# The lower form of the inverse's first level: by a mask and the preceding token's beta in place of sixteen products with the unit matrix

## The chip, the cores and the metric

The kernel runs on one core of one Trainium2 chip. The metric is the device time of one execution in microseconds. Three executions of the kernel before took 4968.78, 4977.33 and 4977.47 us; their median, 4977.33 us, is the time before.

## What is computed

Two transformer layers over 4096 tokens of width 256. Layer 0 adds a gated delta rule attention (16 heads of 64) and a mixture of 16 experts to its input; layer 1 adds a linear attention and a nested attention. Only the delta rule is touched by the change. For each head, with state `S` (64x64) and, per token, key `k`, query `q`, value `v`, log decay `g` and step size `beta = sigmoid(x @ Wb.T)`:

```
Sk    = einsum('bhkv,bhk->bhv', S, k_t)
delta = v_t (x) k_t - Sk (x) k_t
S     = exp(g_t) * S + b_t * delta
o_t   = einsum('bhkv,bhk->bhv', S, q_t)
```

The tokens of a head depend on each other in turn. The kernel takes them in chunks of 64: within a chunk the updates solve a triangular system, so a 64x64 triangular matrix (unit diagonal, off it the products of keys, the decays between two tokens and a beta) has to be inverted for each head and each chunk, and then the state goes from chunk to chunk.

## The kernel before, in words

The program runs in six phases, one after the other: norm and router, projections, delta rule (`phase_delta`), experts, second norm, attention. Each phase gives every engine a list of its own; engines meet only at semaphores, and each works its list strictly in order.

`phase_delta` has 64 chunks of 64 tokens. Two chunks make a couple, `x` = 0 and 1, and there are 32 couples. A tile is 128 partitions by 8 pairs of heads by 64 columns (128x512 f32): a head is a 64x64 square in the upper or the lower half of the partitions, so a product over all heads of a chunk is a block of sixteen matmuls (`heads()`, `each()`); a profile shows such a block as 32 weight loads and 32 matmuls of 64x64.

A round of the loop, `one(post, pre, ahead)` of each engine, works on three couples at once. For `ahead`, SP loads keys, queries, values and running sums of the decays (`load`, L758), and the decays are exponentiated. For `pre` the inverse is built (which needs no state). For `post` the state goes through its two chunks: `residual`, `updates`, `outputs`, `new_state`, then `project`. The loop's body holds two rounds. In all 32 rounds have a `pre`, 31 of them a `post` as well.

The inverse is built by doubling. `inv[x]` holds the inverse in its upper form, the transpose of it is the lower form, and both are needed since a matmul takes its left operand transposed. Level one (within pairs of neighbouring tokens) is made from `upper` by GpSimd: `first_inverse` (L1103) multiplies with the mask `couples` and subtracts from the unit matrix, two operations a chunk. Its lower form was made by TensorE: `first_low` (L819) multiplies `inv[x]` with the unit matrix into `p_low`, one block a chunk, and ScalarE's `keep_low` (L960) copies `p_low` to `inv_low[x]`. Each further level k = 1 to 4 is then, for each chunk: `half` (L825: `upper` by `inv_low` into `p_pre`), `mask_step` (L1038, VectorE, into `step`), `low` (L830: adds to what stands in `p_low`), `up` (L836: into `p_pre`), and then `keep_low` (ScalarE) and `add_up` (L1042, VectorE: `inv` plus `p_pre`). Level five has no lower form. `half(x, k + 1)` waits for the lower form of level k and for `add_up(x, k)`, which frees `p_pre`.

TensorE's order in a round is written out by hand (L875 to L918): keys by keys, residual 0, keys by keys, keys by queries, key rows 0, updates 0, keys by queries, key rows 1, outputs 0, `first_low(0)`, new_state 0, `first_low(1)`, `half(0, 1)`, `half(1, 1)`, residual 1, and then the levels, each `low 0, up 0, low 1, up 1, half 0`, one of updates 1, outputs 1, new_state 1 (levels 1 to 3), `half 1`. The last `up`s stand among two halves of `project`. VectorE's order is at L1052, ScalarE's at L964, GpSimd's at L1130, SP's at L776. `residual(post, 1)` waits for the state that VectorE's `take_state(post, 0)` (L1033) makes from new_state 0.

Of the kernel before, what the change touches and what calls it, by code (L numbers as in the profile page):

```python
# [24 lines left out]
C = 64  # L25
# [24 lines left out]
def shape_constants():  # L50

    p = np.arange(P)
    half, s = p // C, p % C
    t = np.arange(C)
    eye = np.eye(P)

    same_head = (half[:, None] == half[None, :]).astype(float)

    running = same_head * (s[:, None] <= s[None, :])
    tri = (s[:, None] <= t[None, :]).astype(float)  # L60
    future = np.where(tri > 0, 0.0, -1e30)


    doublings = []
    for n in range(LEVELS):
        w = 1 << n
        doublings.append((s[:, None] // (2 * w) == t[None, :] // (2 * w)) * (s[:, None] % (2 * w) >= w) * (t[None, :] % (2 * w) < w) * -1.0)
    couples = (s[:, None] // 2 == t[None, :] // 2) * (s[:, None] % 2 < 1) * (t[None, :] % 2 >= 1) * 1.0
    eye_c = (s[:, None] == t[None, :]).astype(float)
    parts = {  # L70
        "eye": eye, "same_head": same_head, "running": running, "future": future,
        "couples": couples, "doublings": np.concatenate(doublings[1:], 1), "eye_c": eye_c,
        "iota": np.tile(np.arange(NE), (P, 1)).astype(float),
        "head_block": (p[:, None] // DL == p[None, :] // DL).astype(float),
    }
# [567 lines left out]
def phase_delta(nc, g, ctx):  # L643
# [23 lines left out]
    k_t, q_t, v_t, sums = (sb(n, [P, 4, NPAIR, C]) for n in ("k_t", "q_t", "v_t", "sums"))  # L667
# [8 lines left out]
    inv_low = [sb(f"inv_low{x}", W) for x in range(2)]  # L676
    step = [sb(f"step{x}", W) for x in range(2)]
# [19 lines left out]
    wo_in, cleared = sem("wo_in"), sem("cleared")  # L697
    res_d, ress_d, w_d, u_d, udec_d, o_d, ocp_d = (sem(s) for s in ("res", "ress", "w", "u", "udec", "o", "ocp"))
# [56 lines left out]
    def _(sp):  # L755
        sp.dma_start(wo[:], g.given["wo_t"].rearrange("(n p) d -> p n d", p=P)).then_inc(wo_in, 16)

        def load(n, x):  # L758
            r, m = n.ring[x], n.chunk[x]
            for h in range(2):  # L760
                sp.dma_start(sums[h * C:(h + 1) * C, r].rearrange("p n t -> p (n t)"),
                             spread(g.sums_d[bass.ds(m, 1), h, :], [C, NPAIR * C])).then_inc(loaded[r], 16)
            for name, dst in (("k", k_t), ("q", q_t), ("v", v_t)):
                src = g.chunks_d[name][bass.ds(m, 1)].rearrange("a p n -> p (a n)")
                sp.dma_start(dst[:, r].rearrange("p n t -> p (n t)"), src).then_inc(loaded[r], 16)
# [10 lines left out]
        def one(post, pre, ahead):  # L776
            if ahead is None:
                return
            for x in range(2):
                if post is not None:  # L780
                    sp.wait_ge(o_d, post.ended[x])
                load(ahead, x)
            load_rows(ahead)
# [6 lines left out]
    def _(pe):  # L790
# [28 lines left out]
        def first_low(n, x):  # L819
            wait_apart(pe, g, (att_d[x], n.now), (inv1_d[x], n.now))  # L820
            for p, hs in heads():
                last = te.matmul(p_low[x][hs, p, :], inv[x][hs, p, :], g.c("eye_c")[hs, :], start=p == 0, stop=False, skip_group_check=True)
            last.then_inc(lowmm_d[x], 1)

        def half(n, x, k):  # L825
            freed = (rows_d[x], n.now) if k == 1 else (up_d[x], n.level[k - 1])
            wait_apart(pe, g, freed, (lowc_d[x], n.level[k]))
            each(p_pre[x], of(upper[x]), of(inv_low[x])).then_inc(half_d[x], 1)

        def low(n, x, k):  # L830
            wait_apart(pe, g, (step_d[x], n.level[k]))
            for p, hs in heads():
                last = te.matmul(p_low[x][hs, p, :], inv[x][hs, p, :], step[x][hs, p, :], start=False, stop=k == NL - 1, skip_group_check=True)  # L833
            last.then_inc(lowmm_d[x], 1)
# [40 lines left out]
        def one(post, pre, ahead):  # L875
# [15 lines left out]
            if pre is not None:  # L891
                first_low(pre, 0)
            if post is not None:
                new_state(post, 0)
            if pre is not None:
                first_low(pre, 1)
                half(pre, 0, 1)
                half(pre, 1, 1)
# [20 lines left out]

        couples(pe, one)  # L920

    @block.scalar
    def _(act):
# [3 lines left out]
        def grown(n, x):  # L927
# [6 lines left out]
            a.activation(grow[:, r, :, 1:], sums[:, r], ACT.Exp).then_inc(grow_d[x], 1)  # L934
# [25 lines left out]
        def keep_low(n, x, k):  # L960
            act.wait_ge(lowmm_d[x], n.level[k + 1])
            a.activation(inv_low[x][:], p_low[x][:], ACT.Copy).then_inc(lowc_d[x], 1)  # L962

        def one(post, pre, ahead):  # L964
# [7 lines left out]
            if pre is not None:  # L972
                keep_low(pre, 0, 0)
                keep_low(pre, 1, 0)
            if post is not None:
                keep_residual(post, 1)
            for k in range(1, NL):
                if pre is not None:
                    for x in range(2):
                        keep_low(pre, x, k)  # L980
                if post is not None and k == 2:
                    keep_outputs(post, 1)
# [15 lines left out]
    def _(dve):  # L998
        v = nc.vector
        v.memset(state[:], 0.0).then_inc(state_d, 1)  # L1000
        masks = g.c("doublings").rearrange("p (n t) -> p n t", n=NL)

        def decays(n, x):
# [3 lines left out]
            v.tensor_tensor(diff[x][:], sums[:, r], per_pair(g.cum, n.chunk[x]), ALU.subtract).then_inc(diff_d[x], 1)  # L1007
# [7 lines left out]
        def take_upper(n, x):  # L1015
            dve.wait_ge(kk_d[x], n.now)
            dve.wait_ge(relb_d[x], n.now)
# [20 lines left out]
        def mask_step(n, x, k):  # L1038
            dve.wait_ge(half_d[x], n.level[k])
            v.tensor_tensor(step[x][:], p_pre[x][:], over_pairs(masks[:, k - 1, :]), ALU.mult).then_inc(step_d[x], 1)  # L1040

# [10 lines left out]
        def one(post, pre, ahead):  # L1052
# [13 lines left out]
            for k in range(1, NL):  # L1066
                if pre is not None:
                    for x in range(2):
                        add_up(pre, x, k)
# [18 lines left out]
    def _(pool):  # L1088
# [3 lines left out]
        pool.wait_ge(cleared, 2)  # L1092

# [9 lines left out]
        def first_inverse(n, x):  # L1103
# [4 lines left out]
            po.tensor_tensor(inv[x][:], over_pairs(g.c("eye_c")), inv[x][:], ALU.subtract).then_inc(inv1_d[x], 1)  # L1108

# [20 lines left out]
        def one(post, pre, ahead):  # L1130
            if post is not None:
                decay_state(post, 0)
            if pre is not None:
                first_inverse(pre, 0)
                first_inverse(pre, 1)
            if post is not None:
                decay_updates(post, 0)
# [1230 lines left out]
```

## Time and profile before

| what | value |
|---|---|
| median of three executions | 4977.33 us |
| the profiled execution's own time | 4995.25 us |
| its span, first to last instruction | 4993.5 us |
| TensorE busy over the span | 4571.5 us (92%) |
| VectorE, ScalarE, GpSimd busy | 3236.5 (65%), 2104.2 (42%), 1165.6 us (23%) |
| delta rule phase, first to last matmul | about 731.9 to 2435 us |

Busy time of TensorE comes from matmuls whose ends are modelled, so a gap in it is a lower bound of a stall; the starts of weight loads (PEld) are the better clock of where TensorE stands. Behind a row in brackets stands how long the engine was idle before it and what released it.

### The profile page before, as it was taken

How to read it: one execution, taken by the hardware profiler on the slowest of the kernel's cores; microseconds unless marked ns; L12 is line 12 of the kernel's file. 1: busy time of each engine (PE TensorE's matmuls, PEld its weight loads, DVE VectorE, ACT ScalarE, POOL GpSimd, SP SyncE). 2: the span in 40 equal slices, each digit the busy share in tenths (PEclk: the TensorE clock that was granted, in tenths of full speed). 3: DMA queues.
4: the chain of work that ended last, by engine and by line, in shares of the span. 5: the costliest groups of instructions: out<-in, count | busy, mean ns of one | idle time of the engine just before them, and what ended most of it. 6: DMA issues, size and time to landing. Idle time of an engine off the chain costs nothing. (4 is left out here: it accounts for less than half of the span.)

```text
span 4993.5 us, 162520 instructions
## 1 busy us (share of the span) xinstructions
PE 4571.5 (92%) x67085; PEld 2950.8 (59%) x67085; DVE 3236.5 (65%) x5639; ACT 2104.2 (42%) x2965; POOL 1165.6 (23%) x1361
## 2 busy tenths in 40 slices
PE   6777759999999999999997777999999999999998
PEld 6333338999999998998764662444444444444443
DVE  4788874444444444444333896878787878787877
ACT  1566642222222222222133442656565656565654
POOL 1354442322322323223102774000000000000000
PEclk9998979999999999999998997999999999999999
DMA  3421241111111111111223333000000000000000
GB/s 106 137 101 71 80 145 44 44 54 53 47 52 52 52 55 44 52 55 44 64 85 113 106 104 76 8 9 14 17 4 17 4 17 4 17 5 18 9 13 8
DMA packets 201350, 250.07 MB, mean 50 GB/s; under 512 B 52864, under 2 KB 132864, under 8 KB 199968
## 3 DMA queue, kind: packets, MB, share of 16 engines
q1 hardware_dynamic: 180240, 209.29, 13.3%
q0 software_dynamic: 6144, 16.79, 1.1%
q10 hardware_dynamic: 14352, 14.55, 0.9%
q8 instruction: 538, 8.81, 0.7%
q14 instruction: 76, 0.62, 0.0%
HBM read 135.18 MB, written 105.38 MB: 48 GB/s over the span
## 5 line engine op out<-in xcount | busy, mean ns | idle before, releaser
L2154 DVE TENSOR_REDUCE part_max<-p_m 128x1 f32<-128x512 f32 x2118 | 1363.9, 686 | 378.8 <-PE p_m L1996 371.3
L2136 ACT ACTIVATE prob<-p_s 128x1024 f32<-128x1024 f32 x1024 | 1048.6, 1024 | 748.4 <-PE p_s L2060 746.5
L2015 PE MATMUL p_o<-prob,v_one 128*64 128x512 f32 x4096 | 1055.0, 593 | 3.9 <-ACT prob L2136 0.5
L1996 PE MATMUL p_m<-keys,queries 96*64 96x512 f16 x4236 | 661.3, 387 | 28.0 <-DMA keys<-parts_d 20.4
L2060 PE MATMUL p_s<-queries,keys 97*64 97x512 f16 x4096 | 618.9, 380 | 0.0
L2060 PEld LDWEIGHTS p_s<-queries,keys 97*64 97x64 f16 x4096 | 227.9, 109 | 599.4 <-issue 593.9
L1050 DVE TENSOR_TENSOR inv<-inv,pd_pre 128x512 f32<-128x512 f32 x256 | 176.2, 688 | 446.2 <-PE pd_pre L795 446.2
L544 PE MATMUL p_proj<-xn_t_all,proj_w_sb 128*128 (+1 forms) x768 | 390.2, 651 | 78.3 <-ACT raw L570 70.3
L962 ACT ACTIVATE inv_low<-pd_low 128x512 f32<-128x512 f32 x320 | 191.1, 597 | 621.1 <-PE pd_low L833 471.3
L795 PE MATMUL pd_pre<-inv,step 64*64 64x64 f32 x10240 | 395.3, 219 | 30.4 <-issue 27.5
L1996 PEld LDWEIGHTS p_m<-keys,queries 96*64 96x64 f16 x4236 | 238.5, 108 | 311.3 <-DVE part_max L2154 56.5
L1964 POOL TENSOR_TENSOR attn<-o_num,o_inv 32x512 f32<-32x512 f32 x64 | 81.2, 1269 | 1453.6 <-DVE o_inv L2173 1447.1
L795 PEld LDWEIGHTS pd_pre<-inv,step 64*64 64x64 f32 x10240 | 351.0, 135 | 68.8 <-issue 66.9
L2015 PEld LDWEIGHTS p_o<-prob,v_one 128*64 128x64 f32 x4096 | 287.5, 136 | 162.9 <-issue 15.9
L795 PE MATMUL pd_pre<-inv_low,upper 64*64 64x64 f32 x10240 | 367.6, 219 | 11.8 <-issue 11.5
L795 PEld LDWEIGHTS pd_pre<-inv_low,upper 64*64 64x64 f32 x10240 | 340.3, 135 | 18.1 <-issue 15.3
L607 DVE SCALAR_TENSOR_TENSOR conv<-raw,conv_w_sb,conv 128x512 f32<-128x512 f32 x384 | 312.4, 813 | 57.0 <-POOL raw L631 45.3
L544 PEld LDWEIGHTS p_proj<-xn_t_all,proj_w_sb 128*128 128x128 f32 x768 | 155.5, 208 | 304.1 <-issue 178.3
L1040 DVE TENSOR_TENSOR step<-pd_pre,const 128x512 f32<-128x512 f32 x320 | 218.2, 690 | 159.7 <-PE pd_pre L795 157.9
L833 PE MATMUL pd_low<-step,inv 64*64 64x64 f32 x8192 | 298.8, 218 | 2.6 <-issue 2.4
L833 PEld LDWEIGHTS pd_low<-step,inv 64*64 64x64 f32 x8192 | 275.4, 135 | 4.6 <-issue 3.7
L1101 POOL TENSOR_TENSOR upper<-rel,beta 128x512 f32<-128x512 f32 x64 | 66.7, 1042 | 669.2 <-ACT rel L943 669.2
(240 smaller groups left out, 6624.5 us busy)
## 6 DMA issues: line engine op xcount, KB each, us to landing
k_d<-qkv SPq DMA_DIRECT2D x8, 2048.0 KB, 7.5
q_d<-qkv SPq DMA_DIRECT2D x8, 2048.0 KB, 12.3
v_d<-qkv SPq DMA_DIRECT2D x8, 2048.0 KB, 7.3
sums<-sums_d SPq DMA_DIRECT2D x128, 128.0 KB, 2.9
k_t<-k_d SPq DMA_DIRECT2D x64, 256.0 KB, 3.2
q_t<-q_d SPq DMA_DIRECT2D x64, 256.0 KB, 3.4
v_t<-v_d SPq DMA_DIRECT2D x64, 256.0 KB, 4.7
slots_d<-zero ACTq DMA_DIRECT2D x1, 10112.0 KB, 31.9
```

Of the source, the lines that this page charges most:

```text
L544: last = te.matmul(p_proj[j % RING][:], g.proj_w_sb[:, n, c, p * P:(p + 1) * P], g.xn_t[:, c, bass.ds(b * BLK, BLK)], start=c == 0, stop=c ...
L607: v.scalar_tensor_tensor(rows, cols, w, rows, ALU.mult, ALU.add).then_inc(conv_d, 1)
L795: last = te.matmul(out[hs, p, :], lhs(p, hs), rhs(p, hs), start=True, stop=True)
L833: last = te.matmul(p_low[x][hs, p, :], inv[x][hs, p, :], step[x][hs, p, :], start=False, stop=k == NL - 1, skip_group_check=True)
L962: a.activation(inv_low[x][:], p_low[x][:], ACT.Copy).then_inc(lowc_d[x], 1)
L1040: v.tensor_tensor(step[x][:], p_pre[x][:], over_pairs(masks[:, k - 1, :]), ALU.mult).then_inc(step_d[x], 1)
L1050: v.tensor_tensor(inv[x][:] if k < NL else inv_fin[:, n.ring[x]], inv[x][:], p_pre[x][:], ALU.add).then_inc(up_d[x], 1)
L1996: last = te.matmul(p_m[k % 2][x * HALF:(x + 1) * HALF, :], queries[0:ROW, p, hh, at:at + HALF], keys[0:ROW, 2 * p + hh, kb * BLK:(kb + 1) ...
L2015: product = te.matmul(p_o[64 * hh:64 * hh + VW, :], g.v_one[:, j, p, hh:hh + 2, :].rearrange("p a d -> p (a d)"), prob[:, j % 2, hh, :], s ...
L2060: last = te.matmul(p_s[j % 2][x * HALF:(x + 1) * HALF, hh, :], keys[0:KR, 2 * p + hh, at:at + HALF], queries[0:KR, p, hh, :], start=True, ...
L2136: a.activation(prob[:, j % 2], p_s[j % 2][:], ACT.Exp, scale=SCORE_SCALE).then_inc(exp_d, 1)
L2154: v.tensor_reduce(part_max[:, hh * SUB + sub, kb:kb + 1], p_m[k % 2][:], AX.X, ALU.max).then_inc(red_d, 1)
```

## The change

The lower form of level one is no longer taken from the upper form. Its only entries off the diagonal are those of a token and the one before it, in which the decay is the factor of the upper form's own and only the beta is of another place. So VectorE masks the product of keys with itself (`couples_low`, -1 at the places) from `p_pre` into a new tile `low_1[x]`; GpSimd multiplies it by `beta_before`, the beta of the token preceding, and adds the unit matrix.

- TensorE: `first_low` is gone (two blocks a round); `half(0, 1)` stands in its first place, and `half(1, 1)` alone stands between new_state 0 and residual 1. `low(x, 1)` now begins the accumulation in `p_low`.
- VectorE: `take_upper` has the masking ahead of its own operation; `add_low` (levels 1 to 4, ahead of each `add_up`) adds `low_1` and `p_low` into `inv_low`.
- ScalarE: all of `keep_low` is gone (five a chunk); `keep_outputs(1)` follows `keep_residual(1)`.
- GpSimd: `first_low` (two operations a chunk) stands where `first_inverse` was, and `first_inverse` comes after `decay_updates(post, 0)`.
- Once, ahead of the loop: one matmul shifts beta by a token, VectorE copies it, and TensorE and GpSimd wait for that.
- `sums` has two places in place of four, so SP's loads wait for the decays and growths of the couple before.
- The constants have 192 more columns (64 for `couples_low`, 128 for `previous`).

```diff
@@ shape_constants
+    couples_low = (s[:, None] // 2 == t[None, :] // 2) * (s[:, None] % 2 >= 1) * (t[None, :] % 2 < 1) * -1.0
+        "couples_low": couples_low, "previous": (p[:, None] == p[None, :] - 1).astype(float),
@@ phase_delta
+    sums = sb("sums", [P, 2, NPAIR, C])
+    low_1 = [sb(f"low_1{x}", W) for x in range(2)]
+    beta_before = sb("beta_before", [P, NCH, NPAIR])
@@ SP, one
+                if pre is not None:
+                    sp.wait_ge(diff_d[x], pre.now)
+                    sp.wait_ge(grow_d[x], pre.now)
@@ TensorE
-        def first_low(n, x):
-            wait_apart(pe, g, (att_d[x], n.now), (inv1_d[x], n.now))
-            for p, hs in heads():
-                last = te.matmul(p_low[x][hs, p, :], inv[x][hs, p, :], g.c("eye_c")[hs, :], start=p == 0, stop=False, skip_group_check=True)
-            last.then_inc(lowmm_d[x], 1)
-            each(p_pre[x], of(upper[x]), of(inv_low[x])).then_inc(half_d[x], 1)
+            each(p_pre[x], of(upper[x]), of(low_1[x] if k == 1 else inv_low[x])).then_inc(half_d[x], 1)
         def low(n, x, k):
+            if k == 1:
+                wait_apart(pe, g, (inv1_d[x], n.now), (step_d[x], n.level[k]))
...
             if pre is not None:
-                first_low(pre, 0)
+                half(pre, 0, 1)
             if post is not None:
                 new_state(post, 0)
             if pre is not None:
-                first_low(pre, 1)
-                half(pre, 0, 1)
                 half(pre, 1, 1)
...
+        te.matmul(p_a[:].rearrange("p n t -> p (n t)"), g.c("previous"), g.beta[:].rearrange("p c n -> p (c n)"), start=True, stop=True).then_inc(shifted_d, 1)
+        pe.wait_ge(beta_d, 1)
@@ ScalarE
-        def keep_low(n, x, k):
-            act.wait_ge(lowmm_d[x], n.level[k + 1])
-            a.activation(inv_low[x][:], p_low[x][:], ACT.Copy).then_inc(lowc_d[x], 1)
@@ VectorE
+        v.tensor_copy(beta_before[:], p_a[:].rearrange("p n t -> p (n t)").rearrange("p (c n) -> p c n", n=NPAIR)).then_inc(beta_d, 1)
         def take_upper(n, x):
             dve.wait_ge(kk_d[x], n.now)
+            v.tensor_tensor(low_1[x][:], p_pre[x][:], over_pairs(g.c("couples_low")), ALU.mult).then_inc(pairs_d[x], 1)
+        def add_low(n, x, k):
+            dve.wait_ge(lowmm_d[x], n.level[k + 1])
+            v.tensor_tensor(inv_low[x][:], low_1[x][:], p_low[x][:], ALU.add).then_inc(lowc_d[x], 1)
...
                     for x in range(2):
+                        add_low(pre, x, k)
                         add_up(pre, x, k)
@@ GpSimd
+        pool.wait_ge(beta_d, 1)
+        def first_low(n, x):
+            pool.wait_ge(pairs_d[x], n.now)
+            po.tensor_tensor(low_1[x][:], low_1[x][:], per_pair(beta_before, n.chunk[x]), ALU.mult).then_inc(scaled_d[x], 1)
+            pool.wait_ge(scaled_d[x], n.now)
+            po.tensor_tensor(low_1[x][:], over_pairs(g.c("eye_c")), low_1[x][:], ALU.add).then_inc(lowc_d[x], 1)
...
             if pre is not None:
+                first_low(pre, 0)
+                first_low(pre, 1)
+            if post is not None:
+                decay_updates(post, 0)
+            if pre is not None:
                 first_inverse(pre, 0)
                 first_inverse(pre, 1)
-            if post is not None:
-                decay_updates(post, 0)
```

## Rows read from the trace of the kernel before

**Rows 1.** The page's busy times: engine, busy us (share), instructions.
```profile
PE 4571.5 (92%) x67085; PEld 2950.8 (59%) x67085; DVE 3236.5 (65%) x5639; ACT 2104.2 (42%) x2965; POOL 1165.6 (23%) x1361
```
**Rows 2.** Windows: stretch, its us, busy of PE, PEld, DVE, ACT, POOL, clock, DMA.
```profile
785.54:1896.07 1110.53, 1064.26 (x32940) 1009.13 (x32938) 483.32 (x714) 257.19 (x442) 331.63 (x316) 1.00 0.16 51
1526.43:1580.89 54.46, 51.14 (x1576) 48.38 (x1572) 23.03 (x34) 12.26 (x22) 15.81 (x16) 1.00 0.15 49
1580.89:1631.56 50.67, 49.95 (x1574) 47.69 (x1572) 23.01 (x34) 12.23 (x22) 15.78 (x16) 1.00 0.17 53
```
**Rows 3.** Groups of instructions by line, 736 to 2440 us.
```profile
L822 PE MATMUL pd_low<-const,inv 64*64 64x64 f32 x2048 | 73.8, 218 | 1.3 <-POOL inv L1108 1.2
...
L962 ACT ACTIVATE inv_low<-pd_low 128x512 f32<-128x512 f32 x320 | 191.1, 597 | 621.1 <-PE pd_low L833 471.3 <-remote 99.4 <-PE pd_low L822 50.4
L1050 DVE TENSOR_TENSOR inv<-inv,pd_pre 128x512 f32<-128x512 f32 x256 | 176.2, 688 | 446.2 <-PE pd_pre L795 446.2
L1108 POOL TENSOR_TENSOR inv<-const,inv 128x512 f32<-128x512 f32 x64 | 81.8, 1278 | 5.0
L1101 POOL TENSOR_TENSOR upper<-rel,beta 128x512 f32<-128x512 f32 x63 | 65.6, 1042 | 661.2 <-ACT rel L943 661.2
```
**Rows 4.** Waits of PE, 785 to 2380 us: total us, times, longest.
```profile
PE pd_pre L795 <- issue: 54.9, 109, 2.7
```
**Rows 5.** Timeline of weight loads: one gap inside a block.
```profile
1545.01 0.25 PEld L795 LDWEIGHTS pd_pre<-inv,step 64*64 64x64 f32 x6 [0.50 <-issue]
```
**Rows 6.** Timeline of PEld and DVE around both first_low blocks: start us, us, what.
```profile
1526.00 1.06 PEld L822 LDWEIGHTS pd_low<-const,inv 64*64 64x64 f32 x32
1526.93 1.06 PEld L795 LDWEIGHTS pd_b<-u_dec,k_row 64*64 64x64 f32 x32
...
1528.24 0.69 DVE L1036 TENSOR_TENSOR state<-state_dec,pd_b 128x512 f32<-128x512 f32 x1 [3.95 <-PE pd_b L795]
1528.80 2.06 PEld L795 LDWEIGHTS pd_pre<-inv_low,upper 64*64 64x64 f32 x64
...
1530.74 0.25 PEld L845 LDWEIGHTS pd_a<-const,v_t 64*64 64x64 f32 x4
```
**Rows 7.** Timeline at the phase's end, where TensorE waits for VectorE's result.
```profile
2431.49 0.69 DVE L1031 TENSOR_TENSOR u<-pd_b,beta 128x512 f32<-128x512 f32 x1 [4.28 <-PE pd_b L795]
2432.29 0.23 PEld L857 LDWEIGHTS pd_a<-q_t,state 64*64 64x64 f32 x4 [1.05 <-issue]
```
**Rows 8.** Timeline of level four: low 1, up 1, both halves, VectorE's add_up 1.
```profile
1610.98 1.07 PEld L833 LDWEIGHTS pd_low<-step,inv 64*64 64x64 f32 x32
...
1611.91 1.06 PEld L795 LDWEIGHTS pd_pre<-inv,step 64*64 64x64 f32 x32
1612.85 2.18 PEld L795 LDWEIGHTS pd_pre<-inv_low,upper 64*64 64x64 f32 x64
1613.23 0.69 DVE L1050 TENSOR_TENSOR inv<-inv,pd_pre 128x512 f32<-128x512 f32 x1 [1.18 <-PE pd_pre L795]
...
1616.96 0.86 DVE L1007 TENSOR_TENSOR diff<-sums,cum 128x512 f32<-128x512 f32 x1
```
**Rows 9.** Timeline of a round's beginning: what GpSimd waits for.
```profile
1519.77 0.69 DVE L1018 TENSOR_TENSOR upper<-pd_pre,upper 128x512 f32<-128x512 f32 x1 [2.15 <-PE pd_pre L795]
1522.75 0.69 DVE L1031 TENSOR_TENSOR u<-pd_b,beta 128x512 f32<-128x512 f32 x1 [1.25 <-PE pd_b L795]
1523.52 1.06 POOL L1112 TENSOR_TENSOR u_dec<-u,rel 128x512 f32<-128x512 f32 x1 [0.19 <-DVE u L1031]
```
**Rows 10.** Timeline of the phase's beginning.
```profile
731.91 0.69 DVE L1007 TENSOR_TENSOR diff<-sums,cum 128x512 f32<-128x512 f32 x1 [8.90 <-DMA v_t<-v_d]
743.60 1.04 PEld L822 LDWEIGHTS pd_low<-const,inv 64*64 64x64 f32 x32 [1.30 <-issue]
```
**Rows 11.** DMA issues: count, size of one, us to landing.
```profile
const<-constants SPq DMA_DIRECT2D x1, 524.0 KB, 3.7
```

More of the change, by code:

```diff
@@ L665, in phase_delta @@
     TRIPS = (LAST - 3) // 2
-    k_t, q_t, v_t, sums = (sb(n, [P, 4, NPAIR, C]) for n in ("k_t", "q_t", "v_t", "sums"))
+    k_t, q_t, v_t = (sb(n, [P, 4, NPAIR, C]) for n in ("k_t", "q_t", "v_t"))
+    sums = sb("sums", [P, 2, NPAIR, C])
     wo = sb("wo", [P, NPAIR, D])
@@ L697, in phase_delta @@
     wo_in, cleared = sem("wo_in"), sem("cleared")
+    shifted_d, beta_d = sem("shifted"), sem("beta")
+    pairs_d, scaled_d = sem2("pairs"), sem2("scaled")
     res_d, ress_d, w_d, u_d, udec_d, o_d, ocp_d = (sem(s) for s in ("res", "ress", "w", "u", "udec", "o", "ocp"))
@@ L760, in load @@
             for h in range(2):
-                sp.dma_start(sums[h * C:(h + 1) * C, r].rearrange("p n t -> p (n t)"),
+                sp.dma_start(sums[h * C:(h + 1) * C, x].rearrange("p n t -> p (n t)"),
                              spread(g.sums_d[bass.ds(m, 1), h, :], [C, NPAIR * C])).then_inc(loaded[r], 16)
@@ L827, in half @@
             wait_apart(pe, g, freed, (lowc_d[x], n.level[k]))
-            each(p_pre[x], of(upper[x]), of(inv_low[x])).then_inc(half_d[x], 1)
+            each(p_pre[x], of(upper[x]), of(low_1[x] if k == 1 else inv_low[x])).then_inc(half_d[x], 1)
         def low(n, x, k):
-            wait_apart(pe, g, (step_d[x], n.level[k]))
+            if k == 1:
+                wait_apart(pe, g, (inv1_d[x], n.now), (step_d[x], n.level[k]))
+            else:
+                wait_apart(pe, g, (step_d[x], n.level[k]))
             for p, hs in heads():
-                last = te.matmul(p_low[x][hs, p, :], inv[x][hs, p, :], step[x][hs, p, :], start=False, stop=k == NL - 1, skip_group_check=True)
-            last.then_inc(lowmm_d[x], 1)
+                last = te.matmul(p_low[x][hs, p, :], inv[x][hs, p, :], step[x][hs, p, :], start=k == 1 and p == 0, stop=k == NL - 1,
+                                 skip_group_check=True)
+            last.then_inc(lowmm_d[x], 2 if k == 1 else 1)
         def up(n, x, k):
@@ L918, in one @@
                 up(pre, 1, NL)
+        pe.wait_ge(g.const_in, 16)
+        te.matmul(p_a[:].rearrange("p n t -> p (n t)"), g.c("previous"), g.beta[:].rearrange("p c n -> p (c n)"), start=True, stop=True).then_inc(shifted_d, 1)
+        pe.wait_ge(beta_d, 1)
         couples(pe, one)
@@ L933, in grown @@
             act.wait_ge(loaded[r], n.loads)
-            a.activation(grow[:, r, :, 1:], sums[:, r], ACT.Exp).then_inc(grow_d[x], 1)
+            a.activation(grow[:, r, :, 1:], sums[:, x], ACT.Exp).then_inc(grow_d[x], 1)
         def related(n, x):
@@ L971, in one @@
                 keep_outputs(post, 0)
-            if pre is not None:
-                keep_low(pre, 0, 0)
-                keep_low(pre, 1, 0)
             if post is not None:
                 keep_residual(post, 1)
[L977 to L982, printed above, removed]
+                keep_outputs(post, 1)
             if ahead is not None:
@@ L1000, in _ @@
         v.memset(state[:], 0.0).then_inc(state_d, 1)
+        dve.wait_ge(shifted_d, 1)
+        v.tensor_copy(beta_before[:], p_a[:].rearrange("p n t -> p (n t)").rearrange("p (c n) -> p c n", n=NPAIR)).then_inc(beta_d, 1)
         masks = g.c("doublings").rearrange("p (n t) -> p n t", n=NL)
@@ L1006, in decays @@
             dve.wait_ge(loaded[r], n.loads)
-            v.tensor_tensor(diff[x][:], sums[:, r], per_pair(g.cum, n.chunk[x]), ALU.subtract).then_inc(diff_d[x], 1)
+            v.tensor_tensor(diff[x][:], sums[:, x], per_pair(g.cum, n.chunk[x]), ALU.subtract).then_inc(diff_d[x], 1)
             dve.wait_ge(diff_d[x], n.now)
```

## The prediction

> **What bounds the kernel now.** I read four views in this order. The page's busy times first: TensorE is busy for 92% of the span and no other engine for more than 65% [rows 1], so work taken from TensorE should count, if it is taken where TensorE has no slack. Then the windows over the delta rule phase, the only one that the change touches. The reader is to see that VectorE does 714 operations in 1110.53 us and 34 in a single round, so the long window is 21 rounds of 52.88 us each. In it TensorE is busy 1064.26 us (96%), VectorE 483.32 (44%), ScalarE 257.19 (23%), GpSimd 331.63 (30%), at a granted clock of 1.00, which is the level of 2.4 GHz [rows 2]. TensorE sets the pace of the round; the others only have to be in time.
>
> Third, the timeline, for the size of a block of sixteen products. A block starts 0.93 us after the one before it: 1526.00, 1526.93, and 1528.80 after one more between [rows 6]. In those units a round holds 48 blocks: 44.8 us, and `project` takes 3.7 more (two halves of 16 products each 256 columns wide, as the starts behind them show). That is 48.6 us of 52.88, so 4.3 us of each round is not products. Fourth, the waits, for what these 4.3 us are: nearly all is named "issue", 54.9 us on `p_pre` alone in 30 rounds [rows 4], and it falls in the midst of a block, where no semaphore stands: after sixteen loads of one `up` block, a pause of 0.50 us, and the rest of the block behind it [rows 5]. Those pauses vary: one round takes 54.46 us, the next 50.67, with the same work [rows 2]. No row shows TensorE waiting for VectorE or ScalarE for long within the loop.
>
> **The change part by part.** The execution profiled took 4995.25 us (span 4993.5, with 1.75 around it), 17.9 us more than the median of the runs shown. All terms are differences within it; I take them off the median, 4977.33.
>
> TensorE loses two blocks a round, in all 64, 73.8 us of recorded busy time [rows 3]; by starts each is 0.93, so 1.87 us a round. They have nothing beside them on TensorE, and it has no slack there.
>
> What is late next? Take the start S of new_state 0 (1526.93 in the trace). VectorE's `take_state` starts at 1528.24, which is S + 1.31, and takes 0.69, to S + 2.00 [rows 6]. TensorE sees a result of VectorE 0.11 us after its end: 2431.49 + 0.69 = 2432.18, and the waiting block starts at 2432.29 [rows 7]. So residual 1 can start at S + 2.11. Before, three blocks stood between (S + 3.81 = 1530.74, [rows 6]) and hid it. After, `half(1, 1)` alone stands there and ends at S + 1.87. A new wait of 0.24 us a round; queued behind it are residual 1 and all levels. Its bounds are 0 (a pause of "issue" falls on it) and 0.5 us (the late pause of the same kind, [rows 5]). Against it, the pair of halves takes 1.94 us before (1528.80 to 1530.74, [rows 6]), 0.07 over two blocks: the second waits for the copy of the lower form, which is now made far earlier. That goes. Net: 1.87 + 0.07 - 0.24 = 1.70 us a round.
>
> Does the lower form come in time? VectorE's mask of p_pre precedes `take_upper`; by the row of chunk 1 it runs 1519.77 to 1520.46 [rows 9], and `take_upper` ends 0.7 later, near 1521.2. TensorE's key rows 1 needs that only at 1523.20. VectorE is free for `take_updates` at 1522.75 all the same, as `attention(0)` ends near 1521.9. GpSimd then does two operations for that chunk, which the trace does not have; the like ones last 1.04 us (a product with beta spread over a chunk, L1101) and 1.28 (with the unit matrix, L1108) [rows 3]: I take 2.35 with a handover, 1520.55 to 1522.9. `half(1, 1)` wants it at 1527.9. `decay_updates(0)`, behind it on GpSimd, starts at 1523.52 when VectorE's u is there [rows 9], so it isn't moved either. Chunk 0's stand 2.3 us earlier.
>
> The upper form goes to the back of GpSimd's queue: from the end of `decay_updates(0)` at 1524.58, four operations of 1.28 give chunk 0 by 1527.2 and chunk 1 by 1529.8. `low(0, 1)` starts at S + 2.11 + 1.87 = 1530.9 and `low(1, 1)` at 1532.8, so 3.0 us are left for chunk 1. Behind them `grow_queries` and `decay_state(1)` end near 1533.2; the latter's user, `take_state(1)`, is three levels off. Cost nothing; were GpSimd's four operations twice as long, 5.1 us more, the loss would be 2.1 us a round.
>
> VectorE gets eight `add_low` and two masks a round: 10 x 0.69 = 6.9 us (bounds by rows: 0.60, ScalarE's copy of the same tile, [rows 3], and 0.86, a longer operation of this size in the loop [rows 8]; I take 0.69, that of `add_up`, which adds from p_pre in the same way [rows 3]). It goes from 23.0 to 29.9 of some 51 us, 59%. What matters is where they stand: `add_low(1, k)` comes just ahead of `add_up(1, k)`, which gates `half(1, k+1)`. Level four has the least room. `low 1` starts at 1610.98, so VectorE can start its sum 1.32 later (1611.91 to 1613.23 for `up 1`, [rows 8]), at 1612.30, and ends at 1612.99: 0.24 us before `add_up 1` starts in any case at 1613.23. The same 0.24 holds for chunk 0. `mask_step` of the next level waits for `half` and comes later still; in levels 1 to 3 another block stands between the halves, which gives 0.9 us more. Cost 0, bounds 0 and 4 x (0.86 - 0.69) = 0.7 us a round. ScalarE loses 10 copies, 191.1 us in all [rows 3], which no one waited for on TensorE but in that 0.07: worth nothing.
>
> The pauses of "issue": I leave them. If they go with the number of products, 1/24 of 54.9 us or so goes too, 2.3 us. The Trainium skill, Runtime: NRT & Kernel Launch, section Instruction fetch mechanics, says that the sequencer streams its instructions in blocks of its own accord, that this is mostly hidden, and that a taken branch is what stalls. Were the pauses of that kind, none would leave with the products, and the sum would be without those 2.3 us; but this case's trace has pauses far from any branch of the loop (0.50 us inside a block), so it doesn't agree that fetching is hidden, if fetching is what they are, which no row tells.
>
> Once only. The first couple has no `post` and waits for GpSimd even before: 1.30 us ahead of the second `first_low` [rows 10]. Its GpSimd work goes from four to eight operations ahead of `low(1, 1)`: from 738.3, about 9.8 us, so 748.4, where before `low 1` stood at 748.42. I take 0 for this round in place of 1.87 (bounds -1.9 and +2). The shift of beta (one matmul, a copy of about 0.69, two handovers, under 4 us) lies before 731.9, when the first keys land [rows 10]; uncovered it would be 3 us. Constants: 192 x 128 x 4 bytes = 98 KB more at the very start, beside 524 KB that land in 3.7 us [rows 11]: 98/524 x 3.7 = 0.7 us (bounds 0 and 1). SP's new waits ask for decays and growths made a round before; its loads go out on `outputs` as ever. The smaller ring of sums costs 0.
>
> Sum: 31 rounds x 1.70 = 52.7, less 0.7: 52.0 us. 4977.3 - 52.0 = 4925.3 us. On the profiled execution's own scale that is 4943.3.
>
> **The rivals.**
> (a) Partly given back: VectorE's additions come late in some levels, or the pauses grow into the time won, since loads of 1 MB now meet the same products at a quicker pace. Half goes: 0.85 x 31 = 26 us, 4951. For it: the pauses already differ by 3.8 us between two rounds [rows 2]. Against: 0.24 us of room at every sum, by rows.
> (b) No change, 4977: the pace is set by something that TensorE's records hide, the streaming of instructions or a chain through the state. Against it: rounds of 50.67 us exist with 49.95 busy [rows 2].
> (c) Slower: VectorE becomes the bound. Each `add_low` waits at the head of its queue for `low`, and behind it stand `add_up` and `mask_step`. It decides once VectorE is late by over 1.70 us a round, 0.43 a level beyond the 0.24 and, in levels 1 to 3, 0.9 of room. With six to seven operations a level that is 0.69 turned to about 0.9. At 0.95 for each of 42 operations of a tile, VectorE would be 40 us busy in chains that leave gaps of 1.2 us at each handover; I put it at +1 us a round, 31 us: 5008. Against it: the mean of VectorE's sums is 0.688 [rows 3], and the loop's longer ones (0.86, [rows 8]) have both inputs from tiles that no matmul writes, as none of the new ones has.
> (d) The edit doesn't shorten the list: excluded, the L822 records are taken out of it by name.
>
> **How the numbers follow.** Forecast 0.78, (a) 0.10, (b) 0.05, (c) 0.07. The forecast's own range is 4912 to 4940: 31 x (1.94 to 1.20 us), first round's 2 and the pauses' 2.3 us, and some 6 us by which medians of runs differ. For 8 in 10 over all I take 4910 to 4958, which holds (a). About 0.2% (10 us) is what a measurement can tell: faster 0.87, same 0.06, slower 0.07.
>
> **What would show it.** The window of 21 rounds should fall from 52.88 to about 51.2 us a round. No L822; new_state 0 to residual 1 in 2.11 us by starts; VectorE 44 operations a round, each `add_low` at 0.69 and ended before `up`'s result; GpSimd 20 operations; span of the phase 52 us less, the other phases within a few us. It is wrong if `half(1, k+1)` starts over 1.0 us after `up 1`'s end in levels 1 to 4, if `low(x, 1)` waits for GpSimd, or if "issue" grows by more than 20 us.

## The result: 83 us faster, 52 forecast

The changed kernel takes 4894.45 us (median of four runs, 4891.91 to 4906.09) against 4977.40 us of the kernel before; the ratio is 0.9843, 95% interval [0.983, 0.9856], which is 78 us of 4977. The forecast of 4925.3 us had the direction, and missed the size: 31 us more went than it said, and the time lies below its range (4910 to 4958). The two profiled executions lie further apart: 4995.25 us before, which is 17.9 above the median, and 4895.71 after. So the traces differ by 99.5 us, and some 17 us of what they show is not in the 83.

The page of the changed kernel, busy times, answers to [rows 1]: TensorE does 2046 matmul records fewer (the 2048 of `first_low`, two more for the shift of beta), ScalarE 320 fewer, VectorE 321 and GpSimd 128 more.

```profile
PE 4516.1 (92%) x65039; PEld 2896.2 (59%) x65039; DVE 3435.6 (70%) x5960; ACT 1910.9 (39%) x2645; POOL 1311.2 (27%) x1489
```

The windows of the changed kernel, in the columns of [rows 2]. The first holds 924 operations of VectorE at 44 a round, 21 rounds: 49.76 us each, where [rows 2] gave 52.88. So the round of this trace is 3.12 us shorter than that of the trace before, not 1.70.

```profile
785.03:1830.01 1044.98, 1017.16 (x31596) 966.26 (x31594) 617.62 (x924) 131.68 (x232) 426.30 (x400) 1.00 0.17 54
1481.29:1530.64 49.35, 47.94 (x1512) 45.74 (x1508) 29.42 (x44) 6.28 (x12) 20.32 (x20) 1.00 0.17 54
```

The timeline of the changed kernel around new_state 0, which answers to [rows 6]. From new_state 0 (1481.78) to residual 1 (1483.90) are 2.12 us; `take_state` begins 1.31 after new_state 0, and residual 1 begins 0.12 after its end at 1483.78. That is the new wait, as forecast.

```profile
1480.85 1.06 PEld L805 LDWEIGHTS pd_pre<-low,upper 64*64 64x64 f32 x32
1481.78 1.06 PEld L805 LDWEIGHTS pd_b<-u_dec,k_row 64*64 64x64 f32 x32
...
1483.09 0.69 DVE L1036 TENSOR_TENSOR state<-state_dec,pd_b 128x512 f32<-128x512 f32 x1 [3.95 <-PE pd_b L805]
...
1483.90 0.23 PEld L853 LDWEIGHTS pd_a<-const,v_t 64*64 64x64 f32 x4
```

Level four of the changed kernel, which answers to [rows 8]: `add_low 1` starts at 1510.04 and `add_up 1` at 1511.04, 0.32 after VectorE fell idle; the pair of halves and its wait take 2.21 us (1510.70 to 1512.91), against 2.24 (1612.85 to 1615.09 in the trace before). VectorE's additions cost TensorE nothing.

```profile
1510.04 0.69 DVE L1044 TENSOR_TENSOR inv_low<-low,pd_low 128x512 f32<-128x512 f32 x1 [0.18 <-PE pd_low L840]
1510.70 2.14 PEld L805 LDWEIGHTS pd_pre<-inv_low,upper 64*64 64x64 f32 x64
1511.04 0.69 DVE L1054 TENSOR_TENSOR inv<-inv,pd_pre 128x512 f32<-128x512 f32 x1 [0.32 <-PE pd_pre L805]
...
1512.91 1.06 PEld L879 LDWEIGHTS pd_b<-wo,o_t 128*64 128x64 f32 x12
```

Groups of the changed kernel, in the columns of [rows 3]: the operations that the forecast had to price.

```profile
L1044 DVE TENSOR_TENSOR inv_low<-low,pd_low 128x512 f32<-128x512 f32 x256 | 175.9, 687 | 125.1 <-PE pd_low L840 125.1
...
L1120 POOL TENSOR_TENSOR low<-const,low 128x512 f32<-128x512 f32 x64 | 82.3, 1287 | 5.0
...
L1118 POOL TENSOR_TENSOR low<-low,beta_before 128x512 f32<-128x512 f32 x64 | 66.7, 1042 | 78.0 <-DVE low L1016 78.0
```

Where are the other 1.42 us a round? The starts of TensorE's blocks, averaged over 21 rounds of each trace from 850 us on (us between the starts named; "sum" is what the blocks between them need at 0.934 each), seem to put them in one place:

| stretch | sum | before | after | difference |
|---|---|---|---|---|
| new_state 0 to residual 1 | | 3.83 | 2.11 | -1.72 |
| residual 1 to low(0, 1) | 1.87 | 2.35 | 2.08 | -0.27 |
| low(0, 1) to updates 1 | 4.66 | 4.92 | 4.82 | -0.10 |
| updates 1 to outputs 1 | 6.53 | 8.10 | 6.69 | -1.41 |
| outputs 1 to new_state 1 | 7.46 | 7.59 | 8.26 | +0.67 |
| new_state 1 to project | | 8.39 | 8.09 | -0.30 |
| all the rest | | 17.59 | 17.59 | 0 |
| round | | 52.77 | 49.64 | -3.13 |

Nothing was removed between updates 1 and outputs 1. What is missing there are two pauses of "issue" a round, like that of [rows 5]. The waits of TensorE in the changed kernel, as [rows 4] for the one before, show them in the whole: 54.9 us in 109 pauses became 35.0 in 51. The 58 that are missing are about two for each of the 30 rounds. The experiments below show that these two pauses go with the chip that a trace was taken on and not with the change: this stretch is where the traces differ most, and it is not where the 31 us are.

```profile
PE pd_pre L805 <- issue: 35.0, 51, 2.7
```

### The profile page after: what moved, and what is told of

The parts are those of the page before. It is cut to its first block and busy times, and to the rows that moved or that the text cites. A ratio compares the mean times of both kernels' runs of the same rounds, so it can differ in the third digit from the quotient of the medians.

```text
span 4893.9 us, 158526 instructions
## 1 busy us (share of the span) xinstructions
PE 4516.1 (92%) x65039; PEld 2896.2 (59%) x65039; DVE 3435.6 (70%) x5960; ACT 1910.9 (39%) x2645; POOL 1311.2 (27%) x1489
## 5 line engine op out<-in xcount | busy, mean ns | idle before, releaser
L805 PE MATMUL pd_pre<-inv,step 64*64 64x64 f32 x10240 | 372.0, 219 | 4.1 <-issue 2.7
L805 PEld LDWEIGHTS pd_pre<-inv,step 64*64 64x64 f32 x10240 | 339.5, 135 | 30.6 <-issue 29.7
L805 PE MATMUL pd_pre<-inv_low,upper 64*64 64x64 f32 x8192 | 302.4, 219 | 16.5 <-issue 15.5
L805 PEld LDWEIGHTS pd_pre<-inv_low,upper 64*64 64x64 f32 x8192 | 275.8, 135 | 24.8 <-issue 21.6
L1044 DVE TENSOR_TENSOR inv_low<-low,pd_low 128x512 f32<-128x512 f32 x256 | 175.9, 687 | 125.1 <-PE pd_low L840 125.1
```

The costliest lines, as they stand in the source:

```text
L805: last = te.matmul(out[hs, p, :], lhs(p, hs), rhs(p, hs), start=True, stop=True)
L1044: v.tensor_tensor(inv_low[x][:], low_1[x][:], p_low[x][:], ALU.add).then_inc(lowc_d[x], 1)
```

## Experiments

Each ran beside the kernel before, so ratios are compared. The chips differ: the kernel before took 4976.63 us in the group of the runs with 64, 16 and 48 products below (the changed kernel's 48), all on one chip, much as at the result (4977.40). It took 4997 to 5000 us in the three other groups, each on another chip. A round is the mean of 21 by the starts of SP's loads.

**What do the pauses need?** First the scatter. In the kernel before, a pause ends 0.76 us (1545.01) and another 1.51 us (1545.76) after the start of the second of each round's two scatters (1544.25), in all rounds looked at. Its indirect DMA:

```profile
1544.25 0.98 POOL L1127 DMA_INDIRECT slots_d<-rows,place  x1 [0.30 <-issue]
...
1545.76 0.36 PEld L795 LDWEIGHTS pd_pre<-inv,step 64*64 64x64 f32 x9 [0.50 <-issue]
```

```diff
-            for k in range(TOPK):
-                po.indirect_dma_start(g.slots_d[:, :], ...).then_inc(scattered[n.odd], 16)
```

> The kernel before without its 64 scatters of normed rows (left out: the rows of the experts' slots, so that the experts work on zeros). In the kernel before each round has about 1.4 us of pauses in the second up of level two, always 0 to 1.5 us after the second scatter's start; the changed kernel has none there. Scatter theory (the pauses need the scatter): updates 1 to outputs 1 falls from 8.10 to about 6.6 us by starts, in all 31 x 1.4 = 44 us less, ratio to the kernel before about 0.991. Instruction stream theory without the scatter (TensorE would pause there anyway): no change in that stretch, ratio 1.00 within 0.003.

Measured: 0.9961 [0.9947, 0.9975]. Updates 1 to outputs 1 fell to 6.77 us, so the pauses there need the scatter. But outputs 1 to new_state 1 rose from 7.59 to 8.20 and other stretches by 0.5 together: the round lost 0.33 us only, which neither theory had. Pauses that are taken away at one place come back at others. The run took 4977.36 us, where the kernel before took 4997.48 on the same chip: without its scatters it has the time that the kernel before has on the faster chips.

**Do ScalarE's copies matter?** The copies of levels 1 to 4 alone go to VectorE:

```diff
-            a.activation(inv_low[x][:], p_low[x][:], ACT.Copy).then_inc(lowc_d[x], 1)
+            v.tensor_copy(inv_low[x][:], p_low[x][:]).then_inc(lowc_d[x], 1)
```

> The kernel before with the copies of the lower form in levels 1 to 4 made by VectorE (ahead of each add_up) and not by ScalarE; first_low and its copy stay. ScalarE theory (the pauses of 1.4 us come with ScalarE's copy of p_low beside the scatter): they go, updates 1 to outputs 1 falls from 8.10 to about 6.7 us, ratio about 0.991. Stream theory (the pause hangs on which instructions TensorE has reached): TensorE's list is the same, the pauses stay, ratio 1.00 (within 0.003).

Measured: 0.9999 [0.9989, 1.0008]; 8.12 us stayed. The ScalarE theory falls, and the forecast's step that VectorE's additions cost nothing stands by itself.

**TensorE's part alone:**

```diff
-                first_low(pre, 0)
+                half(pre, 0, 1)
...
-                first_low(pre, 1)
-                half(pre, 0, 1)
                 half(pre, 1, 1)
...
-            each(p_pre[x], of(upper[x]), of(inv_low[x]))
+            each(p_pre[x], of(upper[x]), of(inv[x] if k == 1 else inv_low[x]))
```

> The kernel before with TensorE's part of the change alone: first_low and its two copies are left out, half(x, 1) takes inv as it is, and the unit matrix is missing from p_low, so the inverse is another one; ScalarE goes on to copy in levels 1 to 4. My forecast's size for this part: 31 x 1.70 = 53 us, ratio 0.9894, in both theories. ScalarE theory: the 1.4 us of pauses stay, so just that, 0.989. Stream theory: the pauses move or go with it, 53 + 44 us less, ratio 0.981.

Measured: 0.9944 [0.9927, 0.996], which neither theory had. The trace says why: new_state 0 to residual 1 is 2.12 us, as in the changed kernel; 8.08 us stayed behind updates 1; and new pauses (1.90 us in the lines below, another of 0.64 behind them) stand behind the loop's back edge, which comes once in two rounds. In the timeline of this kernel, the start of a round (in the kernel before this stretch has but the first pause):

```profile
1444.93 0.22 PEld L795 LDWEIGHTS pd_pre<-k_t 64*64 64x64 f32 x4 [1.03 <-issue]
1447.05 0.89 PEld L795 LDWEIGHTS pd_pre<-k_t 64*64 64x64 f32 x28 [1.90 <-issue]
```

So TensorE had nearly the same list as in the changed kernel and 52.2 us a round in place of 49.8, of which 0.9 are the pauses behind the scatter. That pointed away from what is computed, to where the list stands.

**The changed kernel without its scatters** (the same edit as in the first run):

> The changed kernel without its 64 scatters (left out: the rows of the experts' slots). If the scatters cost the changed kernel nothing any more, it is as the changed kernel, 0.9843 of the kernel before, within 0.003; if the pauses were only moved to other places (updates 1 to new_state 1 still has 0.8 us over the sum of its blocks), it is faster by up to 31 x 0.9 = 28 us, ratio 0.979.

Measured: 0.9802 [0.9786, 0.9818], a little beyond 0.9843 within 0.003; the round was 49.74 us by the loads' starts, against 49.76 with the scatters. The 0.4% are in neither the loop nor the experts (259.3 us from their first load to their last store, 258.6 with the scatters): the run took 4896.75 us, the changed kernel 4894.45, and it is the kernel before that took 4997.48 here and 4977.40 there. The changed kernel with its scatters was not run on this chip, so what they cost it there stays open.

This run and the first one are on the same chip, and neither has a scatter. They differ by 80.6 us and by 2.81 us a round, so the excess over the forecast's 1.70 is 1.1 us a round here too, with the scatter's pauses out of it.

**Layout.** The kernel before with the change's tiles, ring of sums, SP waits, constants and semaphores, but none of its operations; and with six spare semaphores alone:

```diff
+    for s in range(6):
+        sem(f"spare{s}")
```

> The kernel before with what the change does to places alone: six more semaphores at the same point, sums with two places and SP's two more waits, the three new tiles (unused), 192 more columns of constants. No operation of an engine is added or taken away in the loop. Layout theory (an address or a semaphore's number makes the scatter stop TensorE): updates 1 to outputs 1 falls from 8.10 to 6.7 us, ratio about 0.991. Order theory (what GpSimd, VectorE and TensorE do at that time in the changed kernel) and stream theory: 8.1 us stays, ratio 1.00 within 0.003.

> The kernel before with six unused semaphores ahead of the same ones as in the change, so that all later ones have the changed kernel's numbers. If the numbers do it, 8.10 falls to 6.7 us and the ratio is 0.991; else 1.00 within 0.003.

Measured: 1.0001 [0.9991, 1.0011] and 1.0005 [0.9995, 1.0014]; with the layout 8.08 us stayed. Layout falls, as what takes those pauses away.

**The stream.** Products that nobody uses, once, ahead of the loop, so that all later instructions of TensorE stand further back:

```diff
+        for rep in range(2):
+            for p, hs in heads():
+                te.matmul(p_b[hs, p, :], g.c("eye_c")[hs, :], g.c("eye_c")[hs, :], start=True, stop=True)
```

> The changed kernel with 32 products of 64x64 more ahead of the loop on TensorE (128 recorded instructions; at most 3 us of their own, ahead of the first keys' arrival). Stream theory (where TensorE's instructions are cut into pieces as they are fetched decides where it pauses, and how long): the round changes from 49.64 us by 0.5 us or more, and the pauses stand at other places of the list. Order theory: the round stays at 49.6 (within 0.2), ratio to the kernel before 0.984.

> The kernel before with the same 32 products ahead of the loop. Stream theory: the round changes from 52.77 us by 0.5 us or more, the 1.4 us behind updates 1 go or shrink. Order theory: 52.8 (within 0.2), 8.1 us stays, ratio 1.00.

Measured: 0.9993 [0.9983, 1.0002] for the changed kernel and 1.0040 [1.0027, 1.0053] for the one before. The whole gain was gone, with each operation of the loop as it was. For the kernel before, 8.08 us stayed, which the stream theory had not expected, and the round rose by 0.5 us (53.39), which it had. Of the 97 us between the profiled executions of the changed kernel with and without the products, 75 lie in the delta rule phase and 23 behind the experts, in the attention, whose loops stand further back too. The windows of the changed kernel with 32 products: 52.31 us a round, VectorE, ScalarE and GpSimd as busy as without them:

```profile
783.82:1882.27 1098.45, 1033.68 (x31597) 975.11 (x31595) 617.14 (x924) 131.86 (x232) 426.94 (x400) 1.00 0.16 52
```

And the pauses behind the second scatter are in this trace (8.11 us from updates 1 to outputs 1), at 0.76 and 1.51 us; that need not be the products' doing, as this group ran on another chip than the changed kernel. The first of them:

```profile
1217.42 0.97 POOL L1142 DMA_INDIRECT slots_d<-rows,place  x1 [0.30 <-issue]
1218.18 0.30 PEld L805 LDWEIGHTS pd_pre<-inv,step 64*64 64x64 f32 x6 [0.49 <-issue]
```

**Pieces.** Counted in weight loads, the pauses of the changed kernel stand 127, 125, 380, 632 or 883 apart: 29 of 44 distances are whole multiples of 126 within 2, and most of the others have the back edge between. (In the trace before it is 22 of 95, since the two pauses behind each second scatter stand elsewhere.) So TensorE seems to get its stream in pieces of 126 weight loads with their matmuls, 252 records, and to pause at a piece's edge when the next is late. Timeline of the changed kernel, two of them, 126 loads apart:

```profile
1439.80 0.48 PEld L805 LDWEIGHTS pd_pre<-inv,step 64*64 64x64 f32 x13 [0.60 <-issue]
...
1443.78 0.48 PEld L840 LDWEIGHTS pd_low<-step,inv 64*64 64x64 f32 x14 [0.23 <-issue]
```

The traces can say more than this. Section 3 of their pages has a DMA queue `q8 instruction`, 538 packets of 16 KB before and 522 after. In the windows of 21 rounds of the kernel before, of the changed one, and of the changed one with 16 products (its window stands below), that queue has:

```profile
q8 instruction: 262, 4.29, 1.6%
q8 instruction: 252, 4.13, 1.6%
q8 instruction: 262, 4.29, 1.6%
```

The first is a packet for each 125.7 weight loads, the second for each 125.4. And the pauses follow the packets: a packet of this queue lands at 1438.32 and the pause above ends at 1439.80; the next lands at 1442.39 and the other pause ends at 1443.78. Of the changed kernel's 45 pauses in the 21 rounds (over 0.15 us on weight loads; the one behind the back edge and the 0.38 us at each of the two `up`s among `project` left out) all 45 end 1.17 to 1.61 us after such a landing. In all 17 traces, with the two places behind the scatter left out as well, it is 921 of 1063 within 1.15 to 1.75 us, and packets come some 4 us apart, so chance would give about one in seven. No row names them as the releaser, but the fixed time behind the landing does: TensorE waits for its instructions. A packet behind whose landing TensorE was waiting is called late here. Six in ten of the late packets start within 4 us behind the issue of a chunk's load of `v_t`, where one in six to one in five of all packets do.

The piece theory has its own test: one piece more (64 products) must bring the gain back. The edit is that above with 4, 1 and 3 repeats, and 1 for the kernel before.

> The changed kernel with 64 products ahead of the loop (256 recorded instructions, 128 weight loads; pauses in the changed kernel stand 126 weight loads or a multiple of it apart). Piece theory: the stream stands in its pieces almost as without them, so the round is 49.6 to 50.3 us again and the ratio 0.984 to 0.988. Any other theory of e7 (the added products themselves, a warmer or later start): as e7 or worse, round 52.3, ratio 0.999.

> The changed kernel with 16 products ahead of the loop, a quarter of a piece. Piece theory: a round of its own between 49.5 and 52.5 us, ratio 0.984 to 0.999; which, it does not say. Theory of the added products: a quarter to half of e7's loss, 0.988 to 0.992.

> The changed kernel with 48 products ahead of the loop, three quarters of a piece. Piece theory: 49.5 to 52.5 us a round, ratio 0.984 to 0.999, and the mean over 0, 16, 32 and 48 products is the changed kernel's own worth: by the forecast of 1.70 us a round, 0.989. Theory of the added products: worse than e7, over 0.999.

> The kernel before with 16 products ahead of the loop. Piece theory: a round of 52.0 to 53.8 us (0 and 32 products: 52.77 and 53.50), ratio 0.997 to 1.004; its two rounds of the loop stand nearly half a piece apart (1568 weight loads are 12.4 pieces), so that it can't be as lucky as the changed kernel, whose round is 11.9 pieces. Theory of the added products: 1.002.

Measured: 0.9841 [0.9825, 0.9858] with 64 products, the ratio of the changed kernel itself; twice the 32 products cost nothing, half of them nearly all of the gain. The theory that the added products cost something falls. These three and 48 products (0.9980) ran on one chip, and none of their traces has the pauses behind the scatter. The kernel before with 16 products took 1.0079, a round of 53.99 us: more than the 1.004 and 53.8 that the piece theory allowed. Window of the kernel with 16 products:

```profile
785.21:1880.72 1095.51, 1031.76 (x31596) 982.09 (x31594) 618.12 (x924) 131.80 (x232) 426.41 (x400) 0.98 0.16 52
```

Its granted clock is 0.98 and not 1.00. Once in two rounds TensorE stands still behind the back edge for up to 4.0 us (1.0 to 1.3 in the changed kernel), and in most of these pauses the granted clock falls to 0.50, the level of 1.2 GHz, for 3.4 or 6.8 us. In these lines 32 loads take 1.82 us where such a block takes 1.06 at the higher level. So at this place the loss is of two parts, pauses and clock. Such falls are also in the rounds with TensorE's part alone, with 48 and 56 products after and with 16 before (mean clock 0.99), and not in those of the changed kernel as given or with 64 products. The lines, a pause and the window around it:

```profile
1347.49 1.82 PEld L805 LDWEIGHTS pd_pre<-k_t 64*64 64x64 f32 x32 [3.97 <-issue]
1346.00:1352.80 6.80, 5.28 (x99) 5.31 (x101) 1.29 (x2) 0.00 (x0) 2.32 (x2) 0.50 0.02 5
```

The last three fill the table (48 repeats' edit; for 8 and 56 products half a block):

> The kernel before with 48 products ahead of the loop, the fourth quarter. With it both kernels have four places. If the change is worth 1.70 us a round, as forecast, its mean over the four is 0.9895 of the mean of before; the changed kernel's mean is 0.9952, so before's would be 1.0058 and this run 1.011. If the change is worth nothing without its place, this run is 0.97.

> The changed kernel with 8 products ahead of the loop, an eighth of a piece later. Piece theory: between 0.984 and 0.999, nearer to 0.999 if the good place is narrow; could be the best of all if the place is on its edge now.

> The changed kernel with 56 products ahead of the loop, an eighth of a piece before the good place. Piece theory: between 0.983 and 0.998.

| products ahead of the loop | before: ratio, round us | after: ratio, round us |
|---|---|---|
| 0 | 1, 52.88 | 0.9843 [0.983, 0.9856], 49.76 |
| 8 | | 0.9872 [0.9856, 0.9889], 51.12 |
| 16 | 1.0079 [1.0059, 1.0099], 53.99 | 0.9990 [0.9981, 1.0], 52.17 |
| 32 | 1.0040 [1.0027, 1.0053], 53.39 | 0.9993 [0.9983, 1.0002], 52.31 |
| 48 | 1.0049 [1.0032, 1.0066], 54.12 | 0.9980 [0.9969, 0.9991], 52.15 |
| 56 | | 0.9925 [0.9909, 0.9942], 52.03 |
| 64 | | 0.9841 [0.9825, 0.9858], 49.84 |

For the kernel before with 48 products, 1.011 was expected and 1.0049 came. Over the four places 0, 16, 32, 48 the mean ratio is 1.0042 before and 0.9952 after, a quotient of 0.9910: 45 us. With the 23 us that 32 products cost the changed kernel in the attention taken off, it is some 51. The forecast, 52.0, is close to what the change is worth over places; four of them don't say it to the microsecond. By rounds the means are 53.60 and 51.60, 2.00 us a round or 62 us, but these mix chips, as follows. Both kernels as given stand at the best of the places tried (64 products tie with the changed kernel), and that was luck.

**The pauses behind the scatter.** They stand in every trace with scatters from the three chips on which the kernel before takes 4997 to 5000 us (the runs with copies on VectorE, with `first_low` left out, both of the layout, both with 32 products, the kernel before with 48, the changed one with 8 and 56), and in the trace before, of 4995.25 us. They stand in none of the four traces from the chip on which it takes 4977, and not in the changed kernel's, taken where it takes 4977 too. They make 0.8 to 0.9 us a round. So three of the four rounds in the middle column and one of the four right of it (without 8, 56 and 64) hold them, and the 1.36 us by which 8 products lengthen the round are for the most part these. No kernel was traced on chips of both kinds, so this is inferred from 15 traces with scatters and not from a pair.

**What the place does.** The loop's body is two rounds. By packets of the instruction queue the changed kernel's body needs 24 at 0, 8 and 64 products and 25 at 16, 32, 48 and 56; the kernel before needs 25 at 0 and 26 at 16, 32 and 48. The places with one packet fewer are the faster ones in both kernels.

## Why the prediction was wrong

- "What is late next": right to the hundredth. 2.11 us was worked out from new_state 0 to residual 1, 2.11 is the mean of 21 rounds; the wait of 0.24 us is there. In the run with TensorE's part alone it is 2.12.
- "Does the lower form come in time" and GpSimd's queue: right. `half(0, 1)` starts on the heels of outputs 0 (1480.85), the two new operations take 1.042 and 1.287 us (1.04 and 1.28 taken), and no row of GpSimd holds up TensorE within the loop.
- VectorE's ten operations: right, 0.687 us (`add_low`) and 0.691 us (the mask, L1016) each (0.69 taken), 44 a round, 29.42 us; the run with the copies on VectorE shows eight of them at no cost alone.
- "The pauses of 'issue': I leave them": this step failed. The sum had 0 for them and, as its bound, 2.3 us in all. What the runs showed in their place: without scatters and on the same chip, the pauses behind a late instruction packet are 2.12 us a round in the kernel before (61 in 21 rounds) and 1.06 in the changed one (50). That is 33 us over 31 rounds, and the miss was 31 (26 by the ratio). The 1.41 us between updates 1 and outputs 1 of the table, 44 us, are not the miss: they go with the chip of the trace before.
- How many packets come late depends on where the loop stands in TensorE's instruction stream. An otherwise equal kernel moves by 1.5% with 16 products in front, on one chip, and back with 64. So the best account of the 31 us is no operation but the place at which the changed list happened to fall.
- The reading of the rows had a gap of its own. "Nearly all is named 'issue', 54.9 us" is 1.8 us a round of the 4.3 that were to be explained; the gaps in front of weight loads, a closer measure, are 3.7 us a round. And "if fetching is what they are, which no row tells" overlooked `q8 instruction` in section 3 of the page.
- Why the given place of the changed kernel is the good one is shown in part only. Its round is 1504 weight loads, 11.94 pieces of 126, so a body of two rounds fits in 24 pieces with little to spare, and the body before (3136 loads, 24.9 pieces) in 25; from most places such a body reaches into one more, as the counts of packets show. Why one packet more costs from 0.5 to 2.6 us a round is not shown, and no run set the length of the round by itself.
- The prediction weighed a rule of the Trainium skill, Runtime: NRT & Kernel Launch, section Instruction fetch mechanics, and left it without a verdict. The same section says that the stream comes in blocks of 256 instructions, and here pauses stand 252 records apart, a packet of the instruction queue for each 125.7 weight loads (the 4 or 5 instructions left over would be waits and register instructions, an inference); with it, the edges of blocks are where to look. That crossing an edge is "mostly hidden" holds in this case for four packets in five: the kernel before waited behind 52 of its 262 packets, 1.35 us a round, and again behind the back edge. That a taken branch stalls agrees with the 1.03 to 1.21 us in front of the first block behind the back edge of the kernel before, and with up to 4.0 us there with 16 products.
- Rival (b) named "the streaming of instructions" as a reason for no change. It is a reason for a gain or a loss as large as the forecast itself, and belonged in the range: over the places tried, 1.5% of the time for the changed kernel and 0.8% for the one before.
- "That the pauses fall without a semaphore" was read rightly in the rows; what was missing is the question whether a change of the list's length moves them.

## What to carry to other kernels

When one engine runs a long list without waits and its trace has pauses inside blocks of equal work, count the instructions between pauses. If many are whole multiples of one number, look at the packets of the instruction queue: pauses that end at a fixed time behind a landing are waits for instructions. Then the time of the kernel depends on where its loop stands, and a change that adds or removes instructions on that engine is measured fairly only at several places: here some 45 to 51 of the 78 us are the change and the rest is its place. A few idle products ahead of the loop are the tool for it. And compare two traces only when the unchanged kernel takes the same time on both their chips: here the largest difference between the two traces outside the blocks removed, 1.41 us a round, went with the chips.

## What the runs showed of the hardware

- TensorE's instructions come in DMA packets of 16 KB on a queue of their own, one for each 125 to 126 weight loads with their matmuls in this loop. When one is late TensorE pauses, by 0.15 to 2.5 us, and goes on some 1.4 us after the packet's landing (1.15 to 1.75 in 921 of 1063 pauses of 17 traces). The late packets are sent 4.1 to 5.2 us after the one before them, the others 3.8 to 4.0 (medians of the traces); a late packet itself takes no longer than 1.0 to 1.2 us. Most late ones come while a chunk's load of 1 MB is under way; that the load holds them back is inferred.
- Moving the loop of the changed kernel by 64, 128 or 192 records costs 1.4 to 1.5% of the whole kernel, by 32 records 0.3%, by 256 records nothing. In the kernel before, 64, 128 and 192 records cost 0.8, 0.4 and 0.5%.
- On three of the chips TensorE is let go twice during a scatter of 128 rows of 1 KB by GpSimd, 0.76 and 1.51 us behind the start of the second indirect DMA, with six to nine weight loads after each; in four traces from a fourth chip it doesn't stop there at all. The pauses need the scatter (8.10 to 6.77 us without it). They don't stand behind the landing of an instruction packet, and what TensorE waits for in them no row names.
- Within a pause of 4.0 us behind the back edge the granted clock fell to 0.50 (1.2 GHz), for 6.8 us, and 32 weight loads took 1.82 us in place of 1.06.
